# Node layers of a four-layer graph network on one core: paired blocks, and 64-row products on alternating halves of the PE array

## The reference

```python
# layer 0, behind the normalised sum over neighbours (agg)
h = jnp.einsum('nd,dh->nh', agg, w1) + b1          # 64 -> 64
h = jax.nn.gelu(h, approximate=False)
out = jnp.einsum('nh,hd->nd', h, w2) + b2          # 64 -> 64
x = _layernorm(x + out)
# layer 1 begins with
Z = jnp.einsum('ni,rio->nro', h, fc_weight)        # 64 -> 8 relations x 64, and 2 x 8 scores
# layer 2, rst = (1 + eps) * feat + neigh
h = jax.nn.relu(rst @ W1 + b1)                     # 64 -> 128
out = h @ W2 + b2                                  # 128 -> 64
# layer 3 begins with
hn = (inputs_node @ W_node).reshape(n, H, D)       # 64 -> 64, and 2 x 4 scores
```

## Time and profile before

| | us |
|---|---|
| median of 3 runs | 9300.25 |
| lowest, highest | 9298.95, 9302.06 |
| profiled execution | 9279.53 |
| its span | 9277.80 |
| layer 0's node stage, first load to last keep | 2374.95 to 2546.72 |
| layer 2's node stage, first load to last keep | 6881.75 to 7001.26 |

### The profile page before, as it was taken

The page is one execution under the profiler, slowest core; times in us unless marked ns, Lnnn a source line. Parts: engine busy times, 40 slices in busy tenths (PEclk is TensorE's granted clock), DMA queues, the critical chain, the costliest instruction groups (busy, mean ns, idle before and its releaser), DMA issues. The chain is left out here.

```text
span 9277.8 us, 87408 instructions
## 1 busy us (share of the span) xinstructions
PE 3990.4 (43%) x18719; PEld 3766.0 (41%) x18720; DVE 1374.1 (15%) x2901; ACT 3150.7 (34%) x8574; POOL 6458.9 (70%) x6800
## 2 busy tenths in 40 slices
PE   6456656566714242433433333333341433424334
PEld 6455656565503242433433333333341332424334
DVE  7100000000330110101230000000012211112125
ACT  1344333434314252433114344343420433424320
POOL 1677777777377777777747777777756777777774
PEclk7555555555555555555555555555555555555555
DMA  2222222222221111111111111111113111111111
GB/s 58 92 55 54 52 55 55 55 53 53 64 64 27 27 27 27 27 27 26 27 24 26 26 26 26 26 26 26 26 20 70 31 31 31 31 31 31 31 31 23
DMA packets 312926, 352.81 MB, mean 38 GB/s; under 512 B 155007, under 2 KB 187813, under 8 KB 309323
## 3 DMA queue, kind: packets, MB, share of 16 engines
q0 software_dynamic: 218064, 232.48, 12.8%
q1 hardware_dynamic: 94640, 117.49, 3.9%
HBM read 309.75 MB, written 42.24 MB: 38 GB/s over the span
## 5 line engine op out<-in xcount | busy, mean ns | idle before, releaser
L770 POOL DMA_INDIRECT rows_l<-table,idx_c_l x3328 | 3140.0, 944 | 1309.0 <-issue 1013.6
L951 POOL DMA_INDIRECT rows_a<-table,idx_c_a x3200 | 3053.1, 954 | 1046.8 <-issue 1046.8
L565 PE MATMUL acc_l<-rows_l,hot_l 128*128 128x65 f32 x6656 | 1495.1, 415 | 1960.6 <-DMA rows_l<-table,idx_c_l 1911.3
L565 PEld LDWEIGHTS acc_l<-rows_l,hot_l 128*128 128x128 f32 x6656 | 1467.4, 332 | 1995.6 <-issue 1995.6
L565 PE MATMUL acc_a<-msg_a,hot_a 128*128 128x66 f32 (+1 forms) x6656 | 1485.9, 423 | 435.7 <-DVE msg_a L1048 224.3
L565 PEld LDWEIGHTS acc_a<-msg_a,hot_a 128*128 128x128 f32 x6656 | 1440.3, 331 | 485.6 <-issue 474.3
L699 ACT ACTIVATE dist_l<-iota,neg_c_l 128x128 bf16<-128x128 f32 x3328 | 1052.1, 386 | 31.1 <-PE acc_l L565 25.6
L699 ACT ACTIVATE dist_a<-iota,neg_c_a 128x128 bf16<-128x128 f32 x2816 | 890.1, 386 | 148.6 <-PE acc_a L565 148.6
L905 ACT ACTIVATE score_a<-score_a 128x128 f32<-128x128 f32 (+1 forms) x28 | 13.1, 469 | 2580.4 <-DVE score_a L1017 2580.4
L1085 PE MATMUL work_a<-ident,rows_a 128*128 128x128 f32 (+1 forms) x70 | 22.4, 444 | 2002.9 <-DMA rows_a<-table,idx_c_a 1988.0
L732 ACT COPY idx_c_l<-src_tl 128x16 int32 (+1 forms) x208 | 42.3, 203 | 2416.7 <-PE acc_l L565 2391.0
(11 more groups left out here) (254 smaller groups left out, 2430.6 us busy)
## 6 DMA issues: line engine op xcount, KB each, us to landing
rows_l<-table,idx_c_l POOLq DMA_INDIRECT x3328, 2.4
rows_a<-table,idx_c_a POOLq DMA_INDIRECT x3328, 2.4
feat<-edge_attr SPq DMA_DIRECT2D x25, 1125.0 KB
feat<-edge_attr SPq DMA_DIRECT2D x25, 937.5 KB
table<-stage SPq DMA_DIRECT2D x49, 260.0 KB, 2.0
spread<-zero SPq DMA_DIRECT2D x12, 832.0 KB, 14.1
starts_l<-spread SPq DMA_DIRECT2D x2, 3328.0 KB, 11.6
target<-target_d SPq DMA_DIRECT2D x5, 832.0 KB, 8.7
```

Source lines behind the costliest of these rows:

```text
L565: return nc.tensor.matmul(acc[:, bass.ds(at, row.shape[-1])], hot, row, start=False, stop=True, skip_group_check=True)
L770: pool.indirect_dma_start(rows[:, s, k, 0:D], None, table, bass.IndirectOffsetOnAxis(idx_c[:, s, k:k + 1], 0)).then_inc(gathered[s], 16)
L951: pool.indirect_dma_start(rows[:, u, k, 0:row], None, table, bass.IndirectOffsetOnAxis(idx_c[:, u, k:k + 1], 0)).then_inc(gathered[u], 16)
```

## The change

Blocks of a group are taken in pairs, PAIRS = 4 (the last pair has one block and padding). Buffers that had 64 partitions get 128: `wa`, `ba`, `wb` (where hidden is 64) and `wsum` are held twice, once in partitions 0 to 63 and once in 64 to 127, which takes more loads. One transpose now turns two blocks, 128 nodes by 2 x 64 features, so that even blocks come to lie in partitions 0 to 63 of `h_t` and `x_t` and odd blocks in 64 to 127: four transposes in place of seven, and copies of 128 x 512 in place of 64 x 896. Products with K = 64 take the even blocks on rows 0 to 63 of the array and the odd blocks on rows 64 to 127; in layer 0 the product with `wa` also writes its two parts to partitions 0 to 63 and 64 to 127. The built program holds these places in the array as (0, 0) and (64, 0), or (64, 64). Even and odd blocks write to different banks of `g_ps` and `o_ps`. The activation is two calls of 512 and 384 columns, and the first sum of y two instructions. The projections go in ORDER, even and odd block in turn; the ring of three banks stays.

```diff
+PAIRS = -(-BPB // 2)
...
-                wa = tsb(f"wa_{tag}", [D, hidden])
-                ba = tsb(f"ba_{tag}", [hidden, 1])
-                wb = tsb(f"wb_{tag}", [hidden, D])
+                wa = tsb(f"wa_{tag}", [P, hidden])
+                ba = tsb(f"ba_{tag}", [P, 1])
+                wb = tsb(f"wb_{tag}", [P, D])
...
-                wsum = tsb(f"wsum_{tag}", [D, cols])
-                h = tsb(f"h_{tag}", [P, BPB, D])
-                h_t = tsb(f"h_t_{tag}", [D, BPB * P])
-                g_t = tsb(f"g_t_{tag}", [hidden, BPB * P])
+                wsum = tsb(f"wsum_{tag}", [P, cols])
+                h = tsb(f"h_{tag}", [P, 2 * PAIRS, D])
+                h_t = tsb(f"h_t_{tag}", [P, PAIRS * P])
+                g_t = tsb(f"g_t_{tag}", [P, 2, PAIRS * P])
...
-                t_ps = tps(f"t_ps_{tag}", [D, 2 * BANK])
-                g_ps = tps(f"g_ps_{tag}", [hidden, 2 * BANK])
-                o_ps = tps(f"o_ps_{tag}", [P, BPB * D])
+                t_ps = tps(f"t_ps_{tag}", [P, BANK])
+                g_ps = tps(f"g_ps_{tag}", [P, 2, BANK])
+                o_ps = tps(f"o_ps_{tag}", [P, 2, BANK])
...
+                LOADED = 16 * (3 + 2 * (P // hidden))
                 PRODUCTS = BPB * S
+                ORDER = [(b, m) for j in range(PAIRS) for m in range(S) for b in (2 * j, 2 * j + 1) if b < BPB]
+                DONE = {b: ORDER.index((b, S - 1)) + 1 for b in range(BPB)}
+                NODE_DONE = {b: ORDER.index((b, 0)) + 1 for b in range(BPB)}
+                SIDES = slice(0, D), slice(D, P)
+                WIDTHS = PAIRS * P, (BPB - PAIRS) * P
...
-                        sp.dma_start(wa[:], w_in).then_inc(loaded, 16)
-                        sp.dma_start(ba[:], b_in.unsqueeze(1)).then_inc(loaded, 16)
-                        sp.dma_start(wb[:], w_out).then_inc(loaded, 16)
+                        for n in range(2):
+                            sp.dma_start(wa[SIDES[n], :], w_in).then_inc(loaded, 16)
+                        for n in range(P // hidden):
+                            sp.dma_start(ba[n * hidden:(n + 1) * hidden, :], b_in.unsqueeze(1)).then_inc(loaded, 16)
+                            sp.dma_start(wb[n * hidden:(n + 1) * hidden, :], w_out).then_inc(loaded, 16)
...
-                            dve.wait_ge(o_done, g + 1)
-                            link(nc.vector.tensor_tensor(y[:], o_ps[:].rearrange("p (b f) -> p b f", f=D), xcur[:, here, :], ALU.add))
+                            dve.wait_ge(o_done, 2 * g + 2)
+                            for n in range(2):
+                                link(nc.vector.tensor_tensor(y[:, n::2], o_ps[:, n, 0:WIDTHS[n] // P * D].rearrange("p (b f) -> p b f", f=D),
+                                                             xcur[:, bass.ds(g * BPB + n, WIDTHS[n] // P, 2), :], ALU.add))
...
-                            act.wait_ge(g_done, g + 1)
-                            nc.scalar.activation(g_t[:], g_ps[:, 0:BPB * P], func, bias=ba[:, 0:1]).then_inc(gt_ready, 1)
+                            act.wait_ge(g_done, 2 * g + 2)
+                            for n in range(2):
+                                rs = slice(0, P) if hidden == P else SIDES[n]
+                                nc.scalar.activation(g_t[rs, n, 0:WIDTHS[n]], g_ps[rs, n, 0:WIDTHS[n]], func, bias=ba[rs, 0:1]).then_inc(gt_ready, 1)
...
-                            for b in range(BPB):
-                                last = nc.tensor.transpose(t_ps[:, b * P:(b + 1) * P], h[:, b], ident[:])
+                            for j in range(PAIRS):
+                                last = nc.tensor.transpose(t_ps[:, j * P:(j + 1) * P], h[:, 2 * j:2 * j + 2].rearrange("p b f -> p (b f)"), ident[:])
...
-                                lo, hi = split[m % S]
-                                b = m // S
-                                nc.tensor.matmul(z_ps[:, m % 3, 0:hi - lo], x_t[:, b * P:(b + 1) * P], wsum[:, lo:hi], start=True, stop=True)\
+                                b, half = ORDER[m]
+                                lo, hi = split[half]
+                                rs = SIDES[b % 2]
+                                nc.tensor.matmul(z_ps[:, m % 3, 0:hi - lo], x_t[rs, b // 2 * P:(b // 2 + 1) * P], wsum[rs, lo:hi], start=True, stop=True)\
...
-                            for lo, hi in ((0, BANK), (BANK, BPB * P)):
-                                ins = nc.tensor.matmul(g_ps[:, lo:hi], wa[:], h_t[:, lo:hi], start=True, stop=True)
-                            ins.then_inc(g_done, 1)
+                            for n in range(2):
+                                to = slice(0, P) if hidden == P else SIDES[n]
+                                nc.tensor.matmul(g_ps[to, n, 0:WIDTHS[n]], wa[SIDES[n], :], h_t[SIDES[n], 0:WIDTHS[n]], start=True, stop=True)\
+                                    .then_inc(g_done, 1)
...
-                                ins = nc.tensor.matmul(o_ps[:, b * D:(b + 1) * D], g_t[:, b * P:(b + 1) * P], wb[:], start=True, stop=True)
-                            ins.then_inc(o_done, 1)
+                                rs = slice(0, P) if hidden == P else SIDES[b % 2]
+                                j = b // 2
+                                ins = nc.tensor.matmul(o_ps[:, b % 2, j * D:(j + 1) * D], g_t[rs, b % 2, j * P:(j + 1) * P], wb[rs, :], start=True, stop=True)
+                                if b >= BPB - 2:
+                                    ins.then_inc(o_done, 1)
...
-                sp.dma_start(fc_s[:], fc.rearrange("r i o -> i r o")).then_inc(loaded, 16)
-                sp.dma_start(attn_s[:], attn.rearrange("r k o -> (r k o)").partition_broadcast(D)).then_inc(loaded, 16)
+                for n in range(2):
+                    sp.dma_start(fc_s[n * D:(n + 1) * D], fc.rearrange("r i o -> i r o")).then_inc(loaded, 16)
+                sp.dma_start(attn_s[:], attn.rearrange("r k o -> (r k o)").partition_broadcast(P)).then_inc(loaded, 16)
```

More of the change, by code:

```diff
@@ L1282, in body @@
                             dve.wait_ge(tx_done, g + 1)
-                            nc.vector.tensor_copy(x_t[:], t_ps[:, 0:BPB * P]).then_inc(xt_ready, 1)
-                        inputs(h, 0).then_inc(h_ready, 1)
+                            nc.vector.tensor_copy(x_t[:], t_ps[:, 0:PAIRS * P]).then_inc(xt_ready, 1)
+                        if BPB % 2:
+                            start = linked(dve, w_chain)
+                            start(nc.vector.memset(h[:, BPB:], 0.0))
+                            start(nc.vector.memset(xg[:, BPB:], 0.0))
+                        inputs(h[:, 0:BPB], 0).then_inc(h_ready, 1)
                         turn(0)
@@ L1299, in keep @@
                                 act.wait_ge(z_done, g * PRODUCTS + m + 1)
-                                emit["keep"](z_ps[:, m % 3], m % S, stage, node, g * BPB + m // S, m // S).then_inc(z_kept, 1)
+                                b, half = ORDER[m]
+                                emit["keep"](z_ps[:, m % 3], half, stage, node, g * BPB + b, b).then_inc(z_kept, 1)
                         EARLY = range(0, PRODUCTS // 2)
@@ L1374, in body @@
                                 pe.wait_ge(ht_ready, g + 2)
-                            for b in range(BPB):
-                                ins = nc.tensor.transpose(t_ps[:, b * P:(b + 1) * P], xg[:, b], ident[:])
+                            for j in range(PAIRS):
+                                ins = nc.tensor.transpose(t_ps[:, j * P:(j + 1) * P], xg[:, 2 * j:2 * j + 2].rearrange("p b f -> p (b f)"), ident[:])
                             ins.then_inc(tx_done, 1)
@@ L1545, in build @@
                 tsb, _ = fresh(nc, st)
-                fc_s = tsb("fc_s", [D, R, D])
-                attn_s = tsb("attn_s", [D, R * 2 * D])
-                prod = tsb("prod1", [D, R, D])
-                score_w = tsb("score_w", [D, 2, R])
+                fc_s = tsb("fc_s", [P, R, D])
+                attn_s = tsb("attn_s", [P, R * 2 * D])
+                prod = tsb("prod1", [P, R, D])
+                score_w = tsb("score_w", [P, 2, R])
                 table1_v = table1.rearrange("(b p r) f -> b p (r f)", p=P, r=R)
@@ L1620, in w3_load @@
             def w3_load(sp, loaded):
-                sp.dma_start(wn_s[:], wn).then_inc(loaded, 16)
+                for n in range(2):
+                    sp.dma_start(wn_s[n * D:(n + 1) * D, :], wn).then_inc(loaded, 16)
                 for n, a in enumerate((ak, aq)):
@@ L1630, in w3_compute @@
                 for n in range(2):
-                    link(nc.vector.tensor_tensor(prod3[0:D], wn_s[:], att_s[0:D, n], ALU.mult))
-                    last = nc.vector.reduce_sum(wsum[:, KEY + n * H:KEY + (n + 1) * H], prod3[0:D].rearrange("p (h d) -> p h d", h=H), AX)
+                    link(nc.vector.tensor_tensor(prod3[:], wn_s[:], att_s[:, n], ALU.mult))
+                    last = nc.vector.reduce_sum(wsum[:, KEY + n * H:KEY + (n + 1) * H], prod3[:].rearrange("p (h d) -> p h d", h=H), AX)
                     if n == 0:
@@ L1648, in build @@
```

(2 more changed lines are left out.)

39 lines of the change are left out of this document (20 added, 19 removed).

## The result

| | before | after |
|---|---|---|
| median | 9300.46 | 9228.03 |
| lowest, highest | 9298.95, 9302.06 | 9211.23, 9234.22 |
| profiled execution, its span | 9279.53, 9277.8 | 9211.23, 9209.4 |
| layer 0's node stage, first load to node write | 172.2 | 118.4 |
| its start, steady groups, last group | 23.1, 132.6, 16.5 | 25.4, 82.2, 10.9 |

The ratio is 0.9919, with an interval of 0.9907 to 0.9931: 0.8% faster, 72 us by the medians. I had forecast 9258 and a range from 9247 to 9297. The two node stages hold nearly the whole difference between the profiled executions, -53.7 and -13.7 of -68.4 us. The profiled execution of each kernel was quicker than its median, by 21 us before and by 17 us after.

A forecast was written before the change was run, and what follows sets the result against it. Layer 0 was taken as bound by PE, layer 2 by a ring of short steps. Terms -31 - 4.1 + 0.9 - 8.6 = -42.8 us, put on the median 9300.25, gave 9258, range 9247 to 9297.

The forecast's parts named there:

- rival E: Layer 0: the two busy halves lift the clock, streams and loads halve, about -3.5 us more a group, 9237; chance 0.04.
- Turns (1): Transposes in both layers, 7 to 4 per turn: 0.64 us off each turn.
- Product with wa (2): First product, both layers: the even half's second pass covers the odd half's first, gain 0.86 us.
- Output products (4): Layer 0: weight loads of the two halves go in pairs, -1.47 us, held a little likelier than no gain.
- y (5): y on DVE in two instructions: +0.19 us for a second fixed part.
- Projections (6): Layer 0: three-bank PSUM ring, round 1.9 us, sets 0.63 a product; steady group 22.19 to 17.0, -31 over six.
- Last group (7): Layer 0's last group: shorter transposes, copy and projections, -4.1 us.
- Start (8): Layer 0's start: more loads delay bb and attn (attn's part taken as +2.0), +0.9 us in all.
- Layer 2 (9): Layer 2: steady groups -1.1 us each, -6.7 for six, last group -1.0, start about -0.9; -8.6 together.
- Case B: Layer 0: output products' weight loads still go one after the other, no gain there; total 9267, chance 0.25.
- C: Both layers: products of two halves still run one by one, only the turns count; 9295, chance 0.17.
- D: Layer 0: each change of half empties the array before the next stream; 9321 at 0.2 us per change, chance 0.06.

The follow-up runs named there:

- before_full3: The kernel before, unpaired, with its 64-row products padded with zeros to 128 rows, repeated on another chip: 9232.76, ratio 0.9931 to before.
- after_third: The changed kernel measured once more, unaltered, beside other kernels on one chip: 9236.14, ratio 0.9937 to before.
- ring2: The changed kernel with two PSUM banks for the projections in place of three: 9252.71, ratio 0.997 to before.
- ring5: The changed kernel with five banks for the projections, output products writing into banks the activation has read: 9204.53, ratio 0.9917 to before.
- evens_first: The changed kernel with output products and projections ordered all even blocks, then all odd ones: 9249.44, ratio 0.9965 to before.
- ring5c: The kernel of ring5 (five banks for the projections) once more, beside after_third on one chip: 9220.42, ratio 0.9919 to before.
- before_full: The kernel before, unpaired, with its 64-row products padded with zeros to 128 rows: 11978.22 on a slower chip, ratio 0.9951 to before.
- full_rows: The changed kernel with every product on all 128 rows, the other half's operand zero: 9215.09, ratio 0.9927 to before.

## Why the prediction was wrong

**The step that failed** is rival E: "the clock rises", at a chance of 0.04, with the argument "131 us of unbroken products stayed at 0.50". The observation is right, the conclusion isn't. It shows that being busy didn't lift the clock with these products. It says nothing on a kernel in which the products differ in what they use of the array, and that is just what the change alters. So every term of the sum was priced at 0.50, and the steady groups ran at 0.73. The prediction did name a clock other than 0.50 as a sign of being wrong altogether. The stretch in the earlier trace rows that had 0.99 was dense too; what set it apart from layer 0 was the product, not the share of busy time. before_full3 shows it: same instructions, 128 rows in place of 64, 0.95. That E's price, 9237, lies near the 9228 measured is luck: it took 21 us for a clock that doubles in all six groups, of which about 13 came, and the other terms gave 9 us more than forecast.

**Were the clock at 0.50 throughout**, the forecast would have held, by this estimate from the measured parts. Layer 0's groups at 15.94 (-6.25 six times, -37.5), its start +2.3, its last group as forecast, -4.1; layer 2's start -2.1, its groups at 13.72 (-1.46 six times, -8.8), its last -1.2: -51.4 together, 9249, inside the range, near its lower end. The remaining 17 us (by the profiled executions; 21 by the medians) are mostly the clock's: 13 of them are layer 0's steady groups, 82.2 against 6 x 15.94 = 95.6. The group at 15.94 began at a slightly raised clock; with the 16.19 of after_third at 0.50 it is 15 of them, and 9250.

Step by step, against the group at 0.51 and counted from its transposes at 2464.88:

- *Turns (1)*: right. The product with `wa` loads at 0.80, in after_third's group at 0.50 at 1.04; 1.63 - 0.64 = 0.99 was forecast.
- *Product with wa (2)*: overlap right, gain too small. Activation 2.04 after the first load; 2.43 forecast, 3.29 before. I let the two halves share only one pass; all four loads fall within 0.29 and both halves start together.
- *Gelu (3)*: 1.28 for 1.2.
- *Output products (4)*: right. y starts 2.00 after their first load, where it was 3.41 in the earlier trace rows: -1.41 for -1.47. Of the two ends the one that I held likelier by a little came true. The rule in the Trainium skill (TensorEngine Tiling, Key Properties) that tiles load and multiply in parallel is borne out by the row of 13 loads in 1.56.
- *y (5)*: two instructions over 0.82 to 0.94 for 0.62, +0.2 to +0.3 for +0.19.
- *Projections (6)*: the ring right, as ring2 and ring5 show. Table load at 11.2 (11.9 forecast), next transposes at 15.94 (17.0 forecast); in after_third's group at 0.50, 11.5 and 16.19. The whole of a steady group was -31 in the sum and is -37.5 at this clock, -36 at 0.50. "This load is now the wait that ends last" holds.
- *Last group (7)*: -5.5 for -4.1, at a clock of 0.62.
- *Start (8)*: +2.3 for +0.9. `attn_s` was issued 2.6 later and DVE began 3.0 later: more than the +2.5 that the term had at worst, and than the +2.0 I took.
- *Layer 2 (9)*: -13.7 for -8.6. Groups of 13.72 for 14.1, one at 12.25 (clock 0.64), and a start that gained 2.1 for 0.9.

*Case B and C* fell: loads and streams both overlap. *D* fell: the 13 loads, which belong to both halves in turn, come one per 0.10, with no gap.

**What stays open.** I have not found what exactly lifts the clock. Full rows do it, also with zeros in half of them; alternating halves do it in part (0.60 to 0.67), and less in evens_first (0.53) and ring2 (0.54). The padded kernels show the cause with full rows; that the same cause is at work, in part, where halves alternate is argued from these clocks, not shown. Profiled executions also differ by more than 10 us in stages that no kernel here touches (from layer 0's node write to layer 2's first load, 4334.3 us in after_third and 4344.9 in ring5c); the comparisons of stages leave that out.

## What to carry to other kernels

Look at the granted clock beside the busy share: PE busy 99% at 0.50 is not a PE at its limit, and padding the products of K = 64 with zeros to 128 rows brought as much as the whole pairing (64 and 61 us on one chip, memsets included). Where products of 64 rows can alternate between the halves, loads and streams both overlap, but what you gain then goes to the next ring: count the PSUM banks, a round from load to keep divided by the banks, before and after. When an argument against a rival is an observation of the old kernel, ask whether the change leaves alone the very thing that made it so.

## What the runs showed of the hardware

- The granted clock follows what the products use of the array and not only how long PE is busy: 131.4 of 132.6 us busy at 0.50 with all products on 64 rows (the transposes alone use 128), 100.1 of 107.8 at 0.55 with the halves in turn only now and then, 72.9 of 81.8 with all on 128 rows at 0.95.
- Rows of zeros count: the padding of before_full holds nothing else.
- The two halves are separate streams with a look ahead: twelve loads took 1.84 even where four products of one half stood ahead of the first of the other, and of the two products with `wa` in after the one of 384 columns, the later in the program, begins its second stream at 2466.38, the one of 512 columns at 2466.59. The Trainium skill (TensorE: Matmul & The Clock Gate, Part 3) says that matmuls start and end in the order of the program; this trace disagrees for starts. The increments of the semaphores still follow the order of the program: the record has the 384-column stream end at 2467.22 and the 512-column one at 2467.64, and both increments come behind the later end, at 2467.66 and 2467.70. All groups of after and after_third show the same. So a semaphore rose only when all earlier products were done too.
- Two products on all rows but on different columns overlap too: the four streams with `wa` in full_rows took 1.07 at full clock, the unpaired ones of before_full3, which write to the same columns, 1.72.
